# Attention: wide row sums inverted by VectorE in the first half of each group, compact sums in the second

## The reference, cut to what matters

```python
scores = jnp.einsum('bqhd,bkhd->bhqk', Q, Kp) / jnp.sqrt(jnp.float32(HD))
if causal:
    scores = jnp.where(mask, scores, -jnp.inf)
a = jax.nn.softmax(scores, axis=-1)
o = jnp.einsum('bhqk,bkhd->bqhd', a, V).reshape(Bq, Sq, Dm)
return o @ wo + bo
```

## Time and profile before

| | us |
|---|---|
| median of 3 runs | 1370.2 (1369.88 to 1373.38) |
| the profiled execution | 1373.32 |
| its span, first to last instruction | 1371.5 |
| the attention phase in it, about | 25 to 610 |
| PE, DVE, ACT, POOL busy over the span | 1232.9, 903.2, 956.0, 878.4 |
| TensorE's granted clock, mean | 0.97 |

### The profile page before, as it was taken

The page is one execution under the profiler, slowest core; times in us unless marked ns, Lnnn a source line. Parts: engine busy times, 40 slices in busy tenths (PEclk is TensorE's granted clock), DMA queues, the critical chain, the costliest instruction groups (busy, mean ns, idle before and its releaser), DMA issues. The chain is left out here.

```text
span 1371.5 us, 61953 instructions
## 1 busy us (share of the span) xinstructions
PE 1232.9 (90%) x24094; PEld 1019.3 (74%) x24094; DVE 903.2 (66%) x2219; ACT 956.0 (70%) x2010; POOL 878.4 (64%) x1416
## 2 busy tenths in 40 slices
PE   4999999998999999758999999987888888888997
PEld 2778888777888887537999999954666666676775
DVE  3888888877878777794555555545777878553331
ACT  1777777777788887456788776636777878755553
POOL 2577777776677775306999998857767777203431
PEclk9999999999999999689999999998899999999999
DMA  4233434333222221051222222344222323111221
GB/s 127 73 115 108 121 109 123 116 95 88 77 83 80 83 76 41 18 137 44 66 67 68 66 67 65 69 127 131 74 60 77 82 73 95 49 35 55 69 69 47
DMA packets 138315, 110.52 MB, mean 81 GB/s; under 512 B 17216, under 2 KB 113984, under 8 KB 138176
## 3 DMA queue, kind: packets, MB, share of 16 engines
q1 hardware_dynamic: 129728, 91.22, 22.6%
q0 software_dynamic: 8448, 17.32, 5.4%
HBM read 74.35 MB, written 34.08 MB: 79 GB/s over the span
## 5 line engine op out<-in xcount | busy, mean ns | idle before, releaser
L956 DVE TENSOR_REDUCE at_mx<-at_ps_s 128x16 f32<-128x1024 f32 x128 | 156.0, 1219 | 89.6 <-PE at_ps_s L598 44.9
L851 ACT ACTIVATE at_pt<-at_ps_t 128x1024 f32<-128x1024 f32 x128 | 130.6, 1020 | 55.6 <-PE at_ps_t L619 54.8
L2533 POOL DMA_INDIRECT ex_xg<-x,ex_ti x136 | 149.6, 1100 | 23.5 <-issue 21.9
L844 ACT ACTIVATE at_pr<-at_dd 128x1024 f32<-128x1024 f32 x128 | 135.1, 1056 | 34.5 <-DVE at_dd L964 34.5
L2605 ACT ACTIVATE ex_hg<-ex_ps_h,ex_wt 128x128 f32<-128x128 f32 x544 | 155.1, 375 | 1.2 <-PE ex_ps_y L2564 1.2
L2647 DVE COPY ex_wt<-experts 128x1156 f32 x133 | 102.1, 767 | 80.4 <-DVE ex_y L2653 74.3
L964 DVE TENSOR_TENSOR at_dd<-at_ps_s,at_mx 128x1024 f32<-128x1024 f32 x128 | 153.5, 1201 | 0.1
L2190 POOL DMA_INDIRECT l_yg<-rows,l_sl x128 | 124.4, 972 | 35.5 <-issue 34.1
L2555 PE MATMUL ex_ps_h<-ex_xt,ex_wt 128*128 128x128 f32 x1088 | 145.8, 277 | 1.1 <-ACT ex_xt L2597 0.8
L2564 PE MATMUL ex_ps_y<-ex_wt,ex_hg 128*128 128x128 f32 x1088 | 143.6, 275 | 0.4 <-ACT ex_hg L2605 0.4
L619 PE MATMUL at_ps_t<-ident,at_pr 128*128 128x128 f32 x1024 | 138.9, 279 | 5.2 <-issue 4.2
(11 more groups left out here) (291 smaller groups left out, 3191.4 us busy)
## 6 DMA issues: line engine op xcount, KB each, us to landing
rows<-ex_y SPq DMA_DIRECT2D x136, 64.0 KB
x<-at_ln_out SPq DMA_DIRECT2D x32, 256.0 KB, 3.1
at_kx<-in_xt SPq DMA_DIRECT2D x16, 256.0 KB, 2.7
at_qx<-in_xt SPq DMA_DIRECT2D x16, 256.0 KB, 2.7
at_vin<-in_xt SPq DMA_DIRECT2D x16, 256.0 KB, 2.8
at_xr<-in_x SPq DMA_DIRECT2D x16, 256.0 KB, 3.0
cx<-in_ctx SPq DMA_DIRECT2D x16, 256.0 KB, 3.1
x1t<-at_xt SPq DMA_DIRECT2D x16, 256.0 KB, 3.4
```

Source lines behind the costliest of these rows:

```text
L844: act.activation(pr[:, p], dd[:, p], ACT.Exp, scale=SCALE).then_inc(p_ready, 1)
L851: act.activation(pt[:, 2 * h + p], ps_t[:, :, :, :], ACT.Copy).then_inc(pt_ready, 1)
L956: dve.tensor_reduce(mx[:, p], ps_s[:, :, 4 * p:4 * p + 4, :], AX.X, ALU.max).then_inc(mx_ready, 1)
L2533: pool.indirect_dma_start(out=xg[:, s, :], out_offset=None, in_=x_src, in_offset=bass.IndirectOffsetOnAxis(ap=ti[:, s:s + 1], axis=0)).the ...
```

## The change

In the first half (h = 0) of each group, `values` writes the sums for every row of O: instead of `c.count`, which leads all four sequences into the same 64 columns, a new constant `c.sums` with ones for a head's eight columns leads each sequence's sum into 64 columns of its own, 256 in all. The number and shapes of the matmuls stay. DVE then inverts 128x256 from PSUM to a new tile `rcw`, waits for its own result, and multiplies O, read straight from `ps_o`, by it. Both stand where `recip` of that half stood, ahead of the moments. The half's `spread`, `copy_o`, `widen` and `normalise` are gone. The second half keeps the old way, with single buffers.

```diff
+    c.sums = n.sb("sums", [P, 2, 32])
...
+            dve.memset(c.sums[:, :, :], 0.0)
...
+                    dve.memset(c.sums[64 * j:64 * j + 64, a, 16 * j + 8 * a:16 * j + 8 * a + 8], 1.0)
...
-                                mm = pe.matmul(ps_o[32 * r:32 * r + 32, GT // 2:GT // 2 + SEQ],
-                                               c.count[:, b, f, :],
+                                first = GT // 2 + (SEQ * b if h == 0 else 0)
+                                mm = pe.matmul(ps_o[32 * r:32 * r + 32, first:first + SEQ],
+                                               c.sums[:, f, :] if h == 0 else c.count[:, b, f, :],
...
-                    if prior:
-                        widen(g * 2 - 2, 0)
...
-                        widen(g * 2 - 1, 1)
+                        widen(a.shift(-1))
...
-                    if prior:
-                        copy_o(g * 2 - 2, 0)
...
+                def normalise_wide(a):
+                    quad = a.g * 2
                     dve.wait_ge(pv_ready, quad + 1)
                     if beyond(a.g, 0):
+                        dve.wait_ge(ot_ready, quad)
                         dve.wait_ge(o_ready, a.g)
+                    dve.reciprocal(rcw[:, :], ps_o[:, GT // 2:GT]).then_inc(rc_ready, 1)
+                    dve.wait_ge(rc_ready, quad + 1)
+                    dve.tensor_tensor(ot[:, 0:GT // 2], ps_o[:, 0:GT // 2], rcw[:, :], ALU.mult).then_inc(ot_ready, 1)
...
                     if prior:
-                        recip(g * 2 - 2, 0)
+                        normalise_wide(a.shift(-1))
                     if closing and a.shift(-2).exists():
                         ln.dve_moments(dve, a.shift(-2))
...
                     maximum(g * 2 + 1, 0)
-                    if prior:
-                        normalise(a.shift(-1), 0)
                     subtract(g * 2 + 1, 0)
...
-                    if prior:
-                        spread(g * 2 - 2, 0)
```

More of the change, by code:

```diff
@@ L454, in attention_phase @@
         pt = n.sb("pt", [P, 4, 2, 4, P])
[L455 to L457 removed]
+        rc = n.sb("rc", [P, SEQ])
+        rcw = n.sb("rcw", [P, GT // 2])
+        rcx = n.sb("rcx", [P, QB, SEQ])
+        ov = n.sb("ov", [P, GT // 2])
         ot = n.sb("ot", [P, GT])
@@ L637, in values, with widen @@
                             for r in range(4):
-                                mm = pe.matmul(ps_o[32 * r:32 * r + 32, GT // 2:GT // 2 + SEQ],
-                                               c.count[:, b, f, :],
+                                first = GT // 2 + (SEQ * b if h == 0 else 0)
+                                mm = pe.matmul(ps_o[32 * r:32 * r + 32, first:first + SEQ],
+                                               c.sums[:, f, :] if h == 0 else c.count[:, b, f, :],
                                                pt[:, 2 * h + b // 2, b % 2, r, SEQ * f:SEQ * f + SEQ],
-                                               start=False, stop=(b == QB - 1 and f == 1), skip_group_check=True)
+                                               start=False, stop=((h == 0 or b == QB - 1) and f == 1),
+                                               skip_group_check=True)
                     mm.then_inc(pv_ready, 1)
[L644 to L647, removed]
+                def widen(a):
+                    pe.wait_ge(ov_ready, a.g + 1)
+                    pe.wait_ge(rcx_ready, a.g + 1)
+                    pe.matmul(ps_o[:, GT // 2:GT], c.same[:, :], rcx[:, :, :], start=True,
                               stop=True).then_inc(r_ready, 1)
@@ L787, in _ @@
                 raw_logits(2)
-                widen(last.g * 2, 0)
                 turn_logits(0)
@@ L795, in _ @@
                 logits(3, L2, L2 + GP)
-                widen(last.g * 2 + 1, 1)
+                widen(last)
                 logits(3, L2 + GP, L3 - GP)
@@ L851, in copy_t, with copy_o @@
                     act.activation(pt[:, 2 * h + p], ps_t[:, :, :, :], ACT.Copy).then_inc(pt_ready, 1)
[L853 to L859, removed]
+                def copy_o(a):
+                    act.wait_ge(pv_ready, 2 * a.g + 2)
+                    act.wait_ge(rc_ready, 2 * a.g + 2)
+                    if beyond(a.g, 0):
+                        act.wait_ge(ot_ready, 2 * a.g)
+                    act.activation(ov[:, :], ps_o[:, 0:GT // 2], ACT.Copy).then_inc(ov_ready, 1)
                 def copy_x(a):
@@ L897, in step @@
                     if prior:
-                        copy_o(g * 2 - 1, 1)
+                        copy_o(a.shift(-1))
                     copy_t(g * 2, 0, 1)
@@ L933, in copy_context @@
                                    ACT.Copy).then_inc(cxt_ready, 1)
-                copy_o(last.g * 2, 0)
                 keep_raw()
@@ L938, in _ @@
                 scale_context(1)
-                copy_o(last.g * 2 + 1, 1)
+                copy_o(last)
                 copy_x(last.shift(-1))
@@ L966, in subtract, with recip, normalise @@
                                       ALU.subtract).then_inc(d_ready, 1)
-                def recip(quad, h):
+                def normalise_wide(a):
+                    quad = a.g * 2
                     dve.wait_ge(pv_ready, quad + 1)
[L970 to L976, removed]
                     if beyond(a.g, 0):
+                        dve.wait_ge(ot_ready, quad)
                         dve.wait_ge(o_ready, a.g)
-                    dve.wait_ge(ov_ready, quad + 1)
-                    dve.tensor_tensor(ot[:, GT // 2 * h:GT // 2 * h + GT // 2], ps_o[:, GT // 2:GT], ov[:, h, :],
-                                      ALU.mult).then_inc(ot_ready, 1)
+                    dve.reciprocal(rcw[:, :], ps_o[:, GT // 2:GT]).then_inc(rc_ready, 1)
+                    dve.wait_ge(rc_ready, quad + 1)
+                    dve.tensor_tensor(ot[:, 0:GT // 2], ps_o[:, 0:GT // 2], rcw[:, :], ALU.mult).then_inc(ot_ready, 1)
+                def recip(a):
+                    dve.wait_ge(pv_ready, 2 * a.g + 2)
+                    if beyond(a.g, 0):
+                        dve.wait_ge(rcx_ready, a.g)
+                    dve.reciprocal(rc[:, :], ps_o[:, GT // 2:GT // 2 + SEQ]).then_inc(rc_ready, 1)
+                def normalise(a):
+                    dve.wait_ge(r_ready, a.g + 1)
+                    dve.wait_ge(ov_ready, a.g + 1)
+                    dve.tensor_tensor(ot[:, GT // 2:GT], ps_o[:, GT // 2:GT], ov[:, :], ALU.mult).then_inc(ot_ready, 1)
                 def residual(a):
@@ L1025, in step @@
                     if prior:
-                        recip(g * 2 - 1, 1)
+                        recip(a.shift(-1))
                     subtract(g * 2 + 1, 1)
@@ L1032, in step @@
                     if prior:
-                        normalise(a.shift(-1), 1)
+                        normalise(a.shift(-1))
                     if a.shift(1).exists():
@@ L1106, in _ @@
                     ln.dve_statistics(dve, last.shift(-1), y_ready)
-                recip(last.g * 2, 0)
+                normalise_wide(last)
                 if closing:
@@ L1111, in _ @@
                 copy_raw(1)
-                normalise(last, 0)
                 dve.wait_ge(p_ready, 4 * NG * nl)
@@ L1117, in _ @@
                 set_aside(0, L2)
-                recip(last.g * 2 + 1, 1)
+                recip(last)
                 find(rest, r.top2, 0, L2)
-                normalise(last, 1)
+                normalise(last)
                 keep_one(r.m2, 0, L2)
@@ L1155, in mask_q, with spread @@
                     ins.then_inc(qb_ready, 1)
[L1157 to L1161, removed]
+                def spread(a):
+                    pool.wait_ge(rc_ready, 2 * a.g + 2)
+                    if beyond(a.g, 0):
+                        pool.wait_ge(r_ready, a.g)
+                    pool.tensor_tensor(rcx[:, :, :], rc[:, None, :].broadcast_to([P, QB, SEQ]),
                                        c.own[:, :, None].broadcast_to([P, QB, SEQ]), ALU.mult).then_inc(rcx_ready, 1)
@@ L1200, in step @@
                     if prior:
-                        spread(g * 2 - 1, 1)
+                        spread(a.shift(-1))
                     add_bias(a)
@@ L1210, in _ @@
                 last = At(nl, NG * nl - 1)
-                spread(last.g * 2, 0)
                 if closing:
@@ L1215, in _ @@
                     gain(last.shift(-1))
-                spread(last.g * 2 + 1, 1)
+                spread(last)
                 if closing:
```

## The result

The changed kernel takes 1392.8 us (median of 4 runs, 1390.65 to 1394.75) against 1370.0 for the kernel before (4 runs, 1368.6 to 1373.38). The ratio is 1.0168, with a 95% interval of 1.0137 to 1.0200: slower by 1.7%. The forecast was 1392.7.

The account below looks back on a forecast made before the run. A loop through DVE, POOL and PE was taken to bound the attention steps, beside a nearly full PE. Added delay of 15.1 us in layer 1 and 7.4 in layer 0 gave 1370.2 + 22.5 = 1392.7 us; range 1376 to 1405.

Parts of the forecast that it names:

- The loop and its place: Attention step: DVE's reciprocal and moments, POOL's 1/sqrt to spread, PE's `turn_x` and `widen`, DVE's second `normalise`; periods become 16.9 us.
- R: Length of DVE's new 256-column reciprocal, unknown from the trace: worked out as 1.72 us, taken as 1.75, bounds 0.78 and 2.19.
- Rival 1: DVE's wide reciprocal is proportional to its columns, 2.19 us, each of 23 steps 0.44 longer: 1403 us; chance 0.17.
- rival 3: DVE's wide reciprocal is mostly fixed cost, 0.78 us: 1370 to 1374 us, no change; chance 0.10.
- The delay: POOL's layer norm 1/sqrt starts 2.53 us behind the start of DVE's reciprocal instead of 1.27: 1.26 us later a step.
- Layer 1: Attention loop of layer 1: slack 0, so 1.26 us a step over 12 steps, 15.1 us.
- Layer 0: Attention loop of layer 0: slack 0.59 us, so 0.67 a step over 11 steps, 7.4 us.
- PE's 0.44: One `widen` less a step on PE, 0.44 us, taken as nothing because `project_v` waits for ACT's `copy_k`.
- Rival 4: Faster: PE sets the period and 0.44 us a step comes back, 13.6 us in all: 1356.6 us; chance 0.08.
- The ends taken as 0: Eight periods outside the loops (0, bounds -0.44 and +1.26 each) and the stretch behind the loop (0, -0.9 to +1.2 us).
- The forecast's own sign of being wrong: Among the signs named beforehand: the ends and the change of layer move by more than 3 us.
- Rival 2: The attention step's delay is partly absorbed, or the reciprocal lies nearer 1.3 us: 1382 us (1375 to 1386); chance 0.12.

## Why the prediction was right

- **The loop and its place** held in every step: POOL released by the moments, `turn_x` and `widen` behind it, DVE's second `normalise` last. Shown by the swap that takes the moments out from behind the reciprocal (the loss gone with all work kept) and by the three lengths of the reciprocal. The periods were to be 16.9 and are 17.0.
- **R:** worked out as 1.72, taken as 1.75; measured 1.740. Between 64 and 256 columns it grows by 1.200 us, 6.25 ns a column, and 128 columns lie on the same line within 2 ns. Rival 1 (proportional) and rival 3 (mostly fixed) fell with it, and so did eight cycles a column, by which the Trainium skill's repeat count of 8 (VectorE: DVE Perf Modes, First, the fixed hardware budget) would read: 1.740 us less the 0.156 of the other operations is 6.2 ns a column, about six cycles at the page's 0.96 GHz.
- **The delay:** forecast 1.26, measured 1.35. The step from the last moment to POOL takes 0.16 (442.31 to 442.47), for which I had put 0.04. This is the term of the sum that was too small, and the earlier trace rows had it: the reciprocal ends at 424.89 and POOL's spread starts at 425.05, the same 0.16.
- **Layer 1:** forecast 15.1 us, came to 15.6: the larger delay less 0.05 of slack that I had taken as 0. **Layer 0:** forecast 7.4, came to 8.4 by the same delay, with the slack of 0.59 as read.
- **PE's 0.44 worth nothing in the loops:** shown by the extra matmul, which cost nothing. Rival 4 (faster) needed it to count, and fell. But the price of `copy_k`'s place was underrated. I let PE's idle time of some 1.3 us stand at `turn_x` and `widen`; it stands for the larger part ahead of `project_v` (10.7 us in 9 steps there, 4.9 at `turn_x`). That did not touch the sum: closing the gap at `project_v` gained nothing.
- **The ends taken as 0** were -3.4 us in the two profiles and -1.2 by the medians, and this is where the forecast was lucky: two terms too small by 1.5 us together, and a rest that varies by more than that from one execution to the next. One reason given for the 0 was misread. Of the eight periods outside the loops, said to be 16.5 to 18.5 us and longer than the new loops, the first took 15.8, one between the layers 16.5 and the last 13.8. PE's waits for its instructions were not in the reasoning at all. The forecast's own sign of being wrong, ends that move by more than 3 us, came up just so in the profiles, in a quantity that moved by 10 us without any change of program.
- **Rival 2,** that part of the delay is absorbed, fell for the loops: in layer 1 the three delays are paid within 0.05. What was given back lies outside them.

## What to carry to other kernels

When an instruction grows on an engine with room, ask what is queued behind it and who waits for that; here 1.2 us of added work cost 1.3 us a step at 68% load, and nothing once one short producer stood ahead of it. Read the slack of a loop from the distance between a producer's end and its consumer's start, stretch by stretch: it told 0.6 and 0 for two layers of the same code, and 0.59 and 0.05 were paid out. A gap next to a wait is a place to look, not a loss: the largest one in the changed kernel could be closed without a gain, and paid only when the real bound was gone. And keep apart what a change does to loops, which repeat, from what lies outside them: two profiled executions of the kernel before differ by 10 us, none of it in the loops, and programs differ there as well.

## What had not been expected of the hardware

- Where steps are written out instead of looped, PE stands still at single matmuls for 0.4 to 2.7 us in the attention phase, with no releaser in the trace: 8.3 us in six gaps between the layers in the kernel before, none over 0.4 us in one look at a changed one. All 301 such gaps in the whole spans of the 13 profiles end 1.07 to 1.67 us behind the end of a 16 KB transfer of instructions. The attention phase's loops have no such transfers and no such gaps, and repeat to 0.01 us a period.
- VectorE's float32 reciprocal from PSUM takes 0.540 us for 64 columns, 0.941 for 128 and 1.740 for 256: 6.25 ns a column, six times the 1.04 ns that the product and the maximum take.
